# Layer 2's bias table, repeated 16 times in device memory and read with falling offsets, in place of products with a reversing matrix

## The chip, the cores and the metric

The kernel runs on one core of a Trainium2 chip. The metric is device time in microseconds (us), the median of several runs. TensorE (PE) does matrix products into PSUM, VectorE (DVE), ScalarE (ACT) and GpSimd (Pool) work on SBUF, and SyncE (SP) issues nearly all DMAs.

## The reference

A sequence of four layers is computed for 16 batches of 128 tokens, 256 wide: an attention with a gate (layer 0), an attention of each token to three neighbouring rows of the context (layer 1), a self-attention and a cross-attention with a relative position bias (layer 2), and a state space block with a cross-attention (layer 3). The change concerns only the bias of layer 2:

```python
def rel_pos_bias(emb, num_q, num_k):
    ...
    rel = k_pos[None, :] - q_pos[:, None]
    ...
    bucket = ret + jnp.where(n < max_exact, n, val_large)
    bias = emb[bucket]
    return jnp.transpose(bias, (2, 0, 1))[None]
...
sim = jnp.einsum('bhnd,bhmd->bhnm', q, k)
sim = (sim + rel_pos_bias(rel_emb, n, m)) * SCALE
```

The bias depends on key position minus query position alone, so of each head there are 2 * 128 - 1 = 255 numbers, and query row q holds 128 of them, from place 127 - q on. There are 16 heads in the self-attention ("sa") and 16 in the cross-attention ("ca"), so 32 rows of 255. It is the same for all batches, and the kernel works it out once.

## The kernel before

One batch is one tile of 128 partitions by 256. The work of a batch is cut into four parts (`PART1` is layers 0 and 1, `PART2` the self-attention, `PART3` the cross-attention, `PART4` layer 3), each a list of named stages. Each engine has its own program, and its order is written by hand: `HEAD` for the opening, in which batches 0 to 3 fill the pipeline, `ORDER` for the loop, `TAIL` for the end. In `HEAD` each letter takes the next stage of one part of one batch: "o" of batch 0's part 1, with the stages of `OPENING` in it, "b" part 1 of batch 1, "e" part 1 of batch 2, "a" part 2 of batch 0. An engine goes through its stages in this order and waits at semaphores, so what stands behind a waiting instruction waits too. A matrix product in float32 shows as two matmuls in the profile.

The bias is made in the opening. The stage `bias_rows` multiplies the embedding with a matrix of zeros and ones on TensorE (L591) and VectorE copies the result to 32 partitions of 255 numbers, `rows_at` (L1155). SP writes it to device memory (L523), waits for it, and reads it back (L525) into `skewed` so that partition p gets each row from place p on: offsets that rise with the partition. Wanted are falling ones. So the eight stages `bias0` to `bias7`, put one each behind eight stages of batch 0, multiply a bank of 512 columns with a reversing matrix ("flip", L601) into `Pc` or `Pd`, and VectorE copies the bank to `bias` (L1160).

What stands around it and is named further on:

- SP, in this order: the table's write and read, the loads of the self-attention's weights Wsaq, Wsakv and Wsao (4 MB), then `store_kv(1)` (L471), which writes the keys and values of batch 0 to `kv_rows`, the index and tokens of batch 2, `store_kv` for batch 1, and the weights of the later layers. All are DMAs of one queue.
- Pool, in this order: `gather` (L1528) of batch 0, an indirect DMA that waits until `kv_rows` has been written and takes three neighbouring rows for each token; `rms0` (L1501 and L1502), the reciprocal root for the norm at the end of layer 0; `rms1`.
- Batch 0 in layers 0 and 1, on TensorE and VectorE: W0o, the gate with W0g, the turn of out0 (`back0`), the scaling L1250 that waits for `rms0`, the centre product L677, the turn (`turn1`), W1q, L1265, and then the attention to the three rows on VectorE, from L1272, which needs the gathered rows, to L1287; the turn L568 of its result, ScalarE's copy of it (o1T), W1o and the sum L1295.

Of the kernel before, what the change touches and what calls it, by code (L numbers as in the profile page):

```python
# [7 lines left out]
B, T, D = 16, 128, 256  # L8
P = 128
# [3 lines left out]
H2, HD2 = 16, 64  # L13
# [7 lines left out]
BUCKETS = 32  # L21
UNIT = 1024
BANK = 512
HU = UNIT // T
# [5 lines left out]
F32 = mybir.dt.float32  # L30
# [7 lines left out]

_SETUP = [("buckets", 2 * T - 1), ("flip", P)]

# [41 lines left out]
def bias_constants():  # L82

    d = np.arange(2 * T - 1) - (T - 1)
    n = np.abs(d)
    far = 8 + sum((n * n >= 64 * 2 ** k).astype(int) for k in range(1, 8))
    bucket = 16 * (d >= 0) + np.where(n < 8, n, far)
    c = np.zeros((P, SETUP_W), np.float32)  # L90
    c[:BUCKETS, SETUP_AT["buckets"][0]:SETUP_AT["buckets"][1]] = np.arange(BUCKETS)[:, None] == bucket[None, :]
    c[:, SETUP_AT["flip"][0]:SETUP_AT["flip"][1]] = np.eye(P)[::-1]
    return c
# [16 lines left out]

FLIPS = 2 * 2 * HU * T // BANK
OPENING = PART1[:2] + ["bias_rows", "fold1"] + PART1[2:]
for _g, _stage in enumerate(("attn0", "gate0", "back0", "center0", "turn1", "near_q", "near_k", "turn_o1")):
    OPENING.insert(OPENING.index(_stage) + 1, f"bias{_g}")

# [11 lines left out]
HEAD = {  # L127
    "PE": "obooobobooboooobobobobooooboooobooobeeabbeabaaebaebeaecdeddadacdaedacecdcdeccdecececdecegigfihfgifghgihgifighfgifiihfffihgifgffhgihiihfhifif",
    "Activation": "oooboobobobobobbobobaeebaaebeedaecadadeacaddccededcceccdcefgfgifghgfiifhigfighgifihigfighhfhihfif",
    "DVE": "oobooboobobbboooooooooobooooobooeaeabebbeaebbbeabddadaaddedacdeccecceceeeedecihifhgifiifhgffigfggfgffifhffifhhffihiifiiigihf",  # L130
    "Pool": "oooboobobbaaebedadceeexdgfhifhffiiiih",
# [15 lines left out]
def merged(order, own, parts):  # L147
# [14 lines left out]

    "prep_exp", "prep_done", "bias_ps", "bias_sb", "skewed_in",

# [23 lines left out]
def build(nc, tokT, ctx, idx, pad, cols, rows, consts, setup, rel, w0_q, w0_k, w0_v, w0_o, w0_g, w1_q, w1_kv, w1_o,  # L188
          wsa_q, wsa_kv, wsa_o, wca_q, wca_kv, wca_o, wm_in, wm_out, w3_q, w3_k, w3_v, w3_o, bias_rows, kv_rows, kv_rows2, out):
    with ExitStack() as stack:  # L190
# [110 lines left out]

        GW = 2 * 2 * HU * T
        skewed = A4[:, 0:GW]
        rows_at = A4[0:2 * H2, GW:GW + 2 * T - 1]
        set_at = A4[:, GW + 2 * T:GW + 2 * T + SETUP_W]
        rel_at = A4[0:BUCKETS, GW + 2 * T + SETUP_W:GW + 2 * T + SETUP_W + 2 * H2]

# [145 lines left out]
        def _(sp):  # L453
# [65 lines left out]
            for m in work1:  # L519
                for a in (0, EDGE + T):  # L520
                    sp.dma_start(m.kv_rows.ap()[a:a + EDGE], Q2["sa"][0:EDGE, 0:2 * D]).then_inc(sem["kv_out"], 16)
            sp.wait_ge(sem["bias_sb"], 1)
            sp.dma_start(bias_rows.ap(), rows_at).then_inc(sem["skewed_in"], 16)  # L523
            sp.wait_ge(sem["skewed_in"], 16)
            sp.dma_start(skewed.rearrange("p (h k) -> p h k", k=T),  # L525
                         bass.AP(tensor=bias_rows, offset=0, ap=[[1, P], [2 * T - 1, 2 * H2], [1, T]])).then_inc(
                             sem["skewed_in"], 16)
            weights("wsa_in", zip(W2["sa"], (wsa_q, wsa_kv, wsa_o)))
# [31 lines left out]
        def _(pe):  # L560
# [27 lines left out]
            def bias_table(t):  # L588
# [3 lines left out]
                          stop=True).then_inc(sem["bias_ps"], 1)  # L592

            def bias_part(g):
                def run(t):
                    if g == 0:
                        pe.wait_ge(sem["skewed_in"], 2 * 16)
                    if g >= 2:
                        pe.wait_ge(sem["bias_sb"], g)
                    a = SETUP_AT["flip"]  # L600
                    pe.matmul((Pc, Pd)[g % 2], set_at[:, a[0]:a[1]], skewed[:, g * BANK:(g + 1) * BANK], start=True,  # L601
                              stop=True).then_inc(sem["bias_ps"], 1)
                return run


# [289 lines left out]
            def project3(t):  # L895
# [4 lines left out]
            stages = {  # L900
                "bias_rows": [bias_table], **{f"bias{g}": [bias_part(g)] for g in range(FLIPS)},
                "kv0": [project0],
# [206 lines left out]
        def _(dve):  # L1109
# [46 lines left out]

            def bias_part(g):
                def run(t):
                    dve.wait_ge(sem["bias_ps"], g + 2)
                    dve.tensor_copy(bias[:, g // 4, g % 4 // 2, g % 2 * BANK:(g % 2 + 1) * BANK],  # L1160
                                    (Pc, Pd)[g % 2]).then_inc(sem["bias_sb"], 1)
                return run

            def held():

                dve.sem_inc(sem["dve_chain"], 1)
                steps[0] += 1

            def softmax_low(t, L, w, p, scores, extra):

                need_unit(t, f"{L}_scores", w)
                held()
                for h in range(HU):
                    at = slice(h * T, (h + 1) * T)
                    ins = dve.tensor_tensor_reduce(p[:, at], scores[:, at], extra(h), 1.0, TOP, ALU.add, ALU.min,  # L1175
                                                   sm(part_of(t, L), "nm", w * HU + h, w * HU + h + 1))
                    if h % (HU // 2) == HU // 2 - 1:
                        ins.then_inc(sem[f"{L}_lows"], 1)
# [261 lines left out]
            def result3(t):  # L1440
# [5 lines left out]
            stages = {  # L1446
                "bias_rows": [bias_table], **{f"bias{g}": [bias_part(g)] for g in range(FLIPS)},
                "inputs": [inputs], "kv0": [project0],
# [236 lines left out]
```

## Time and profile before

| | |
|---|---|
| runs | 1284.43, 1286.72 and 1281.44 us, median 1284.43 |
| span of the profiled execution | 1284.9 us (no time of it is listed beside the span) |
| busy | PE 1225.8, DVE 883.1, ACT 770.2, POOL 332.6 us |
| TensorE's mean granted clock | 0.985 of full speed |
| device memory | 37.64 MB read, 6.35 MB written |

The span goes from the first instruction to the last. Busy times overlap, since the engines run side by side; what counts is the chain of work that ends last.

### The profile page before, as it was taken

What the parts mean: (1) busy time and instruction counts of PE and PEld (TensorE: products, weight loads), DVE (VectorE), ACT (ScalarE), POOL (GpSimd) and SP (SyncE); (2) the same over time, 40 slices, a digit from 0 to 9 for tenths busy, and PEclk for the clock granted to TensorE, in tenths of its full rate; (3) what the DMA queues carried; (4) which work ended last, traced back from release to release, by engine and by line L of the source; (5) the groups of instructions that cost most, each with busy time, mean ns of one, the idle gap of its engine ahead of it and who ended that gap; (6) DMA issues with size and microseconds to landing.
All of it is one profiled execution on the core that took longest, in us unless ns stands there. A gap on an engine that the chain in (4) does not pass through costs nothing.

```text
span 1284.9 us, 27988 instructions
## 1 busy us (share of the span) xinstructions
PE 1225.8 (95%) x9644; PEld 988.3 (77%) x9644; DVE 883.1 (69%) x3414; ACT 770.2 (60%) x2658; POOL 332.6 (26%) x750
## 2 busy tenths in 40 slices
PE   5899899999999999999999999999999999999887
PEld 3568687788788787788788788878878787788665
DVE  4674667687686768678686867768676876836464
ACT  3447457565766756576775757576575655655533
POOL 2111441312314141222314131231414123112150
PEclk9899899999999999999999999999999999999899
DMA  7730001001010100001010100101010010000000
GB/s 219 290 120 13 34 2 43 13 11 44 0 49 4 49 4 25 28 8 45 0 49 4 44 9 8 45 0 49 4 49 4 16 37 34 5 6 1 9 1 13
DMA packets 28620, 44.67 MB, mean 35 GB/s; under 512 B 4716, under 2 KB 20620, under 8 KB 28056
## 3 DMA queue, kind: packets, MB, share of 16 engines
q1 hardware_dynamic: 26264, 31.42, 7.4%
q0 software_dynamic: 2304, 12.58, 2.7%
q8 instruction: 29, 0.48, 0.1%
q14 instruction: 23, 0.19, 0.0%
HBM read 37.64 MB, written 6.35 MB: 34 GB/s over the span
## 4 chain that ended last, share of the span: by engine, by line
PE 89%; DVE 5%; ACT 2%; issue 1%; DMA 1%; POOL 1%; SPq 0%; DVEq 0%; POOLq 0%
PE psum L574 57%; PE psum L568 11%; PE psum L759 5%; PE psum L782 4%; PE psum L625 3%; PE psum L821 2%; PE psum L876 1%; PE psum L836 1%; PE psum L647 1%; PE psum L916 1%; PE psum L677 1%; ACT A L938 1%; PE psum L891 1%; DVE A L1175 1%; ACT A L930 0%
## 5 line engine op out<-in xcount | busy, mean ns | idle before, releaser
L938 ACT ACTIVATE A<-A,small_ 128x128 f32<-128x128 f32 x640 | 248.5, 396 | 49.6 <-DVE small_ L1175 49.6
L930 ACT ACTIVATE A<-psum 128x512 f32<-128x512 f32 (+2 forms) x231 | 155.7, 700 | 173.7 <-PE psum L568 152.9
L568 PE MATMUL psum<-cst,A 128*128 128x128 f32 x888 | 131.5, 281 | 20.8 <-DVE A L1287 6.9
L568 PEld LDWEIGHTS psum<-cst,A 128*128 128x128 f32 x888 | 101.9, 143 | 43.8 <-issue 14.5
L938 ACT ACTIVATION_READ_ACCUMULATOR A<-A,small_ 128x1 f32 x640 | 125.0, 195 | 0.0
L1501 POOL TENSOR_SCALAR small_<-small_ 128x1 f32<-128x1 f32 x96 | 22.6, 236 | 370.1 <-DVE small_ L1189 203.7
L1175 DVE CUSTOM_DVE_ANT_0 A<-psum,cst 128x128 f32<-128x128 f32 x256 | 56.7, 287 | 66.6 <-PE psum L625 66.4
L1175 DVE CUSTOM_DVE_ANT_0 A<-psum,bias 128x128 f32<-128x128 f32 x264 | 58.4, 287 | 63.3 <-PE psum L759 63.3
L1185 DVE TENSOR_TENSOR A<-A,small_ 128x1024 f32<-128x1024 f32 x80 | 98.3, 1229 | 2.7
L938 ACT ACTIVATE sa_p<-sa_p,small_ 128x128 f32<-128x128 f32 x248 | 96.1, 398 | 4.3 <-DVE small_ L1175 4.3
L1366 DVE SCALAR_TENSOR_TENSOR A<-psum,half_cw,A 128x127 f32<-128x127 f32 (+2 forms) x270 | 70.7, 344 | 32.0 <-ACT A L1062 32.0
L1615 POOL TENSOR_TENSOR small_<-small_,neg_half 128x1 f32<-128x1 f32 x16 | 9.0, 565 | 316.8 <-DVE small_ L1408 316.8
L574 PEld LDWEIGHTS psum<-A,Wmi 128*128 128x128 f32 x600 | 69.3, 192 | 9.2 <-issue 9.1
L1175 DVE DVE_READ_ACCUMULATOR2_ANT small_<- 128x1 f32 x896 | 74.8, 83 | 0.1
L574 PE MATMUL psum<-A,Wmi 128*128 128x128 f32 x600 | 74.4, 279 | 0.0
L1502 POOL TENSOR_TENSOR small_<-small_,neg_half 128x1 f32<-128x1 f32 x96 | 59.2, 617 | 8.0
L946 ACT ACTIVATE A<-psum,col 128x128 f32<-128x128 f32 x94 | 38.0, 462 | 36.8 <-PE psum L568 36.7
L574 PE MATMUL psum<-A,Wcaq 128*128 128x128 f32 x480 | 56.3, 275 | 0.0
L574 PE MATMUL psum<-Wcao,A 128*128 128x256 f32 x240 | 56.2, 388 | 0.0
L574 PE MATMUL psum<-A,Wcakv 128*128 128x128 f32 x480 | 56.2, 275 | 0.0
L574 PEld LDWEIGHTS psum<-A,Wcaq 128*128 128x128 f32 x480 | 54.9, 192 | 0.5 <-ACT A L946 0.5
L574 PEld LDWEIGHTS psum<-A,Wcakv 128*128 128x128 f32 x480 | 54.8, 192 | 0.1
(314 smaller groups left out, 2886.8 us busy)
## 6 DMA issues: line engine op xcount, KB each, us to landing
kv_rows<-A SPq DMA_DIRECT2D x16, 256.0 KB
IN<-in_tokT SPq DMA_DIRECT2D x15, 256.0 KB, 2.6
A<-bias_rows SPq DMA_DIRECT2D x1, 2048.0 KB, 10.0
Wsakv<-in_wsa_kv SPq DMA_DIRECT2D x1, 2048.0 KB, 11.6
Wcakv<-in_wca_kv SPq DMA_DIRECT2D x1, 2048.0 KB, 12.8
ctx_end<-in_tokT SPq DMA_DIRECT2D x16, 128.0 KB, 2.2
out<-x_out SPq DMA_DIRECT2D x16, 128.0 KB, 1.7
IN<-in_ctx SPq DMA_DIRECT2D x15, 128.0 KB, 2.0
```

The lines of the kernel that those rows point to most:

```text
L568: mm = pe.transpose(out[:, c * P:(c + 1) * P], src[:, c * P:(c + 1) * P], ident)
L574: mm = pe.matmul(out, lhs[k], rhs[k], start=(k == 0), stop=(k == len(lhs) - 1))
L625: mm = pe.matmul((m.Pa, m.Pb)[r], m.q0o[rows, w * T:(w + 1) * T], m.bk0[rows, :], start=True, stop=True)
L759: mm = pe.matmul(X[:, at:at + T], Q2[S][64 * e:64 * e + 64, a:a + T], K2[S][64 * e:64 * e + 64, a:a + T], start=True, stop=True)
L782: mm = pe.matmul(X[64 * e:64 * e + 64, at:at + T], V2[S][:, h * HD2:(h + 1) * HD2], (Q2, K2)[w][S][:, (4 * e + c) * T:(4 * e + c + 1) * T] ...
L930: return act.activation(out, in_, ACT.Copy)
L938: ins = act.activation(p[:, h * T:(h + 1) * T], p[:, h * T:(h + 1) * T], ACT.Exp, scale=-1.0, bias=sm(part, "nm", w * HU + h, w * HU + h + 1),
L946: ins = act.activation(out[:, k * T:(k + 1) * T], src[:, k * T:(k + 1) * T], ACT.Identity, bias=pc(shift, k), scale=pc(scale, k))
L1175: ins = dve.tensor_tensor_reduce(p[:, at], scores[:, at], extra(h), 1.0, TOP, ALU.add, ALU.min, sm(part_of(t, L), "nm", w * HU + h, w * HU ...
L1185: dve.tensor_tensor(heads(p), heads(p), each(rc, T), ALU.mult).then_inc(sem[f"{L}_probs"], 1)
L1366: ins = dve.scalar_tensor_tensor(to, m.P_4[:, c * T:(c + 1) * T - d], half_cw[:, c * TAPS + TAPS - 1 - d:c * TAPS + TAPS - d], to, ALU.mul ...
L1502: pool.tensor_tensor(out, t, neg_half[:, 0:1], ALU.pow).then_inc(sem[name], 1)
```

## The change

The table is written to device memory 16 times over, so that each of the 32 rows stands there 16 times one behind another (`WRAP` = 16). A row is 255 numbers long. Going from partition to partition by 254 numbers, which is one copy further and one number back, gives offsets that fall with the partition, for 16 partitions at a time. Eight DMAs, one for each group of 16 partitions, put the bias straight into `bias`. The reversing matrix, the eight products and the eight copies are gone, and VectorE waits for the eight DMAs ahead of the first softmax of the self-attention.

```diff
-_SETUP = [("buckets", 2 * T - 1), ("flip", P)]
+_SETUP = [("buckets", 2 * T - 1)]
...
-FLIPS = 2 * 2 * HU * T // BANK
+WRAP = 16
 OPENING = PART1[:2] + ["bias_rows", "fold1"] + PART1[2:]
-for _g, _stage in enumerate(("attn0", "gate0", "back0", "center0", "turn1", "near_q", "near_k", "turn_o1")):
-    OPENING.insert(OPENING.index(_stage) + 1, f"bias{_g}")
...
-            sp.dma_start(bias_rows.ap(), rows_at).then_inc(sem["skewed_in"], 16)
-            sp.wait_ge(sem["skewed_in"], 16)
-            sp.dma_start(skewed.rearrange("p (h k) -> p h k", k=T),
-                         bass.AP(tensor=bias_rows, offset=0, ap=[[1, P], [2 * T - 1, 2 * H2], [1, T]])).then_inc(
-                             sem["skewed_in"], 16)
+            sp.dma_start(bias_rows.ap(), rows_at.unsqueeze(1).to_broadcast([2 * H2, WRAP, 2 * T - 1])).then_inc(sem["table_out"], 16)
+            sp.wait_ge(sem["table_out"], 16)
+            flat = bias[:].rearrange("p a w n -> p (a w) n").rearrange("p a (h k) -> p (a h) k", k=T)
+            for a in range(0, P, WRAP):
+                sp.dma_start(flat[a:a + WRAP], bass.AP(tensor=bias_rows, offset=T - 1 - a,
+                                                       ap=[[2 * T - 2, WRAP], [WRAP * (2 * T - 1), 2 * H2], [1, T]])).then_inc(
+                                                           sem["bias_in"], 16)
             weights("wsa_in", zip(W2["sa"], (wsa_q, wsa_kv, wsa_o)))
...
             def softmax_low(t, L, w, p, scores, extra):
 
                 need_unit(t, f"{L}_scores", w)
+                if L == "sa" and w == 0 and t.first:
+                    dve.wait_ge(sem["bias_in"], P // WRAP * 16)
...
-    bias_rows = nc.dram_tensor("bias_rows", (2 * H2, 2 * T - 1), F32)
+    bias_rows = nc.dram_tensor("bias_rows", (2 * H2, WRAP, 2 * T - 1), F32)
```

The functions `bias_part` of TensorE and VectorE are taken out with their stages, and `HEAD` loses eight letters "o" for each of the two engines. The other stages keep their order.

Line numbers shift with the change (L525 becomes L522, L494 L489, L471 L466, L574 L571). On SP's queue, between the small stores that clear the edges of `kv_rows` and the tokens of batch 2, there stood:

```order
L523 DMA bias_rows<-A 32x255
L525 DMA A<-bias_rows 128x32x128
L494 DMA Wsaq<-in_wsa_q 128x2x1024
L494 DMA Wsakv<-in_wsa_kv 128x2x2048
L494 DMA Wsao<-in_wsa_o 128x8x256
L471 DMA kv_rows<-A 128x512
```

and now, with the semaphores that SP waits for:

```order
L518 DMA bias_rows<-A 512x1x255 [waits bias_sb]
L522 DMA bias<-bias_rows 16x32x128 [waits table_out]
L522 DMA bias<-bias_rows 16x32x128 x7
L489 DMA Wsaq<-in_wsa_q 128x2x1024
L489 DMA Wsakv<-in_wsa_kv 128x2x2048
L489 DMA Wsao<-in_wsa_o 128x8x256
L466 DMA kv_rows<-A 128x512 [waits kv1_sb]
```

One read of 128 partitions has become eight of 16, all ahead of the three Wsa loads and of the store of keys and values.

On TensorE, from batch 1's product with W1kv (its `kv1`) to the gate product of batch 1, there stood:

```order
L574 MATMUL psum<-W1kv,A 128x512 [waits folded]
L574 MATMUL psum<-W1kv,A 128x512
L601 MATMUL psum<-A 128x512 [waits bias_sb]
L677 MATMUL psum<-A,cst 128x256 [waits y0]
L601 MATMUL psum<-A 128x512 [waits bias_sb]
L568 MATMUL psum<-cst,A 128x128 [waits x1]
L568 MATMUL psum<-cst,A 128x128
L574 MATMUL psum<-A,W0o 128x128 [waits l0_osb,w0_in]
L574 MATMUL psum<-A,W0o 128x128 x3
L601 MATMUL psum<-A 128x512 [waits bias_sb]
L574 MATMUL psum<-W1q,A 128x256 [waits x1gT]
L574 MATMUL psum<-W1q,A 128x256
```

and now:

```order
L571 MATMUL psum<-W1kv,A 128x512 [waits folded]
L571 MATMUL psum<-W1kv,A 128x512
L662 MATMUL psum<-A,cst 128x256 [waits y0]
L565 MATMUL psum<-cst,A 128x128 [waits x1]
L565 MATMUL psum<-cst,A 128x128
L571 MATMUL psum<-A,W0o 128x128 [waits l0_osb,w0_in]
L571 MATMUL psum<-A,W0o 128x128 x3
L571 MATMUL psum<-W1q,A 128x256 [waits x1gT]
L571 MATMUL psum<-W1q,A 128x256
```

The three products with the reversing matrix are gone from between; nothing else has moved.

## Rows read from the trace of the kernel before

**Rows 1.** The page: span, TensorE's busy time, and what the DMAs moved in 40 slices.

```profile
span 1284.9 us, 27988 instructions
...
PE 1225.8 (95%) x9644; PEld 988.3 (77%) x9644; DVE 883.1 (69%) x3414; ACT 770.2 (60%) x2658; POOL 332.6 (26%) x750
...
GB/s 219 290 120 13 34 2 43 13 11 44 0 49 4 49 4 25 28 8 45 0 49 4 44 9 8 45 0 49 4 49 4 16 37 34 5 6 1 9 1 13
```

**Rows 2.** The instructions of L601 and of L1160: durations (ns), starts (us).

```profile
L601 PE MATMUL psum<-A x16: 592/592/1061, 42.0 to 64.1; 128*128 128x512 f32 x16
...
L1160 DVE COPY bias<-psum x8: 684/692/693, 43.1 to 65.2; 128x512 f32<-128x512 f32 x8
```

**Rows 3.** The chain of work up to 110 us: start us, us, what.

```profile
5.62 5.16 DMA A<-in_rel
...
42.19 0.86 PE psum L601 x2
...
55.53 0.87 PE psum L601 x2
...
60.23 0.69 DVE bias L1160
...
63.45 1.71 PE psum L601 x2
...
66.90 0.43 DVE x L1295
...
75.92 11.64 PE psum L574 x76
```

**Rows 4.** Timeline of SP from 20 us: start us, us, operation.

```profile
20.07 0.31 SPq L523 DMA_DIRECT2D bias_rows<-A  x1
21.54 0.39 SPq L525 DMA_DIRECT2D A<-bias_rows  x1
...
28.04 0.49 SPq L494 DMA_DIRECT2D Wsao<-in_wsa_o  x1
42.42 0.34 SPq L471 DMA_DIRECT2D kv_rows<-A  x1
```

**Rows 5.** DMA issues from 20 to 46 us: last number, us to landing.

```profile
A<-bias_rows SPq DMA_DIRECT2D x1, 2048.0 KB, 10.0
...
Wsao<-in_wsa_o SPq DMA_DIRECT2D x1, 1024.0 KB, 14.5
...
bias_rows<-A SPq DMA_DIRECT2D x1, 31.9 KB, 1.5
...
A<-kv_rows,near_at POOLq DMA_INDIRECT x1, 5.0
```

**Rows 6.** DMA issues from 40 to 60 us, the same columns.

```profile
IN<-in_tokT SPq DMA_DIRECT2D x1, 256.0 KB, 2.7
```

**Rows 7.** The page's DMA issues, medians over the whole span.

```profile
out<-x_out SPq DMA_DIRECT2D x16, 128.0 KB, 1.7
```

**Rows 8.** Timeline of Pool from 40 us; in brackets idle time before, and releaser.

```profile
45.38 1.23 POOL L1528 DMA_INDIRECT A<-kv_rows,near_at  x1 [18.60 <-DMA kv_rows<-A]
49.51 0.18 POOL L1501 TENSOR_SCALAR small_<-small_ 128x1 f32<-128x1 f32 x1 [2.90 <-ACT A L978]
```

**Rows 9.** Timeline of all engines from 43 to 76 us.

```profile
48.62 1.88 PE L574 MATMUL psum<-W1kv,A 128*128 128x512 f32 x4
...
57.03 0.95 DVE L1272 TENSOR_TENSOR A<-A 128x768 f32<-128x768 f32 x1
...
62.76 0.69 PE L568 MATMUL psum<-cst,A 128*128 128x128 f32 x2 [3.73 <-DVE A L1287]
```

**Rows 10.** Windows of 2 us: busy us (count) by engine, granted clock, DMA share, GB/s.

```profile
60.00:62.00 2.00, 0.00 (x0) 0.00 (x0) 1.93 (x4) 0.00 (x0) 0.00 (x0) 1.00 0.96 400
...
64.00:66.00 2.00, 2.00 (x5) 1.21 (x4) 1.56 (x4) 0.00 (x0) 0.00 (x0) 0.50 1.07 370
...
68.00:70.00 2.00, 2.00 (x16) 1.95 (x14) 1.46 (x5) 0.00 (x0) 1.74 (x5) 0.79 1.00 396
```

More of the change, by code:

```diff
@@ L91, in bias_constants @@
     c[:BUCKETS, SETUP_AT["buckets"][0]:SETUP_AT["buckets"][1]] = np.arange(BUCKETS)[:, None] == bucket[None, :]
-    c[:, SETUP_AT["flip"][0]:SETUP_AT["flip"][1]] = np.eye(P)[::-1]
     return c
@@ L127 @@
 HEAD = {
-    "PE": "obooobobooboooobobobobooooboooobooobeeabbeabaaebaebeaecdeddadacdaedacecdcdeccdecececdecegigfihfgifghgihgifighfgifiihfffihgifgffhgihiihfhifif",
+    "PE": "oboooboboobooobobbobooboboobeeabbeabaaebaebeaecdeddadacdaedacecdcdeccdecececdecegigfihfgifghgihgifighfgifiihfffihgifgffhgihiihfhifif",
     "Activation": "oooboobobobobobbobobaeebaaebeedaecadadeacaddccededcceccdcefgfgifghgfiifhigfighgifihigfighhfhihfif",
-    "DVE": "oobooboobobbboooooooooobooooobooeaeabebbeaebbbeabddadaaddedacdeccecceceeeedecihifhgifiifhgffigfggfgffifhffifhhffihiifiiigihf",
+    "DVE": "oobooboobobbboooooboooboeaeabebbeaebbbeabddadaaddedacdeccecceceeeedecihifhgifiifhgffigfggfgffifhffifhhffihiifiiigihf",
     "Pool": "oooboobobbaaebedadceeexdgfhifhffiiiih",
@@ L161 @@
     "const_in", "w0_first", "w0_in", "w1_in", "wsa_in", "late_in",
-    "prep_exp", "prep_done", "bias_ps", "bias_sb", "skewed_in",
+    "prep_exp", "prep_done", "bias_ps", "bias_sb", "table_out", "bias_in",
     "kv0", "q0", "l0_o", "attnT", "gateT", "out0", "x1c", "x1T", "kv1", "q1", "o1T", "y1",
@@ L300, in build @@
         pad_at = xc[:, 0:T].bitcast(I32)
[L302 to L306, printed above, removed]
+        rows_at = A4[0:2 * H2, 0:2 * T - 1]
+        set_at = A4[:, 2 * T:2 * T + SETUP_W]
+        rel_at = A4[0:BUCKETS, 2 * T + SETUP_W:2 * T + SETUP_W + 2 * H2]
         def C(name, p=P):
@@ L592, in bias_table @@
                           stop=True).then_inc(sem["bias_ps"], 1)
[L594 to L603, printed above, removed]
             def project0(t):
@@ L900, in _ @@
             stages = {
-                "bias_rows": [bias_table], **{f"bias{g}": [bias_part(g)] for g in range(FLIPS)},
+                "bias_rows": [bias_table],
                 "kv0": [project0],
@@ L1155, in bias_table @@
                 dve.tensor_scalar(rows_at, Pd[0:2 * H2, 0:2 * T - 1], -HD2 ** -0.5, None, ALU.mult).then_inc(sem["bias_sb"], 1)
[L1157 to L1162, printed above, removed]
             def held():
@@ L1446, in _ @@
             stages = {
-                "bias_rows": [bias_table], **{f"bias{g}": [bias_part(g)] for g in range(FLIPS)},
+                "bias_rows": [bias_table],
                 "inputs": [inputs], "kv0": [project0],
```

## The prediction

> **What bounds the kernel now.** I read the page first: the span is 1284.9 us and TensorE is busy for 95% of it [rows 1]. The change touches only the opening, so the next view is the chain of work up to 110 us. From 75.92 on it is TensorE with hardly a break: there a shift of the start is carried to the end, neither grown nor made good. Before that the chain is one of short steps on TensorE, VectorE, ScalarE and Pool, with loads between them, and the removed work stands on it: five pieces of L601, 0.86 or 0.87 us each, the first at 42.19 and the last at 55.53, one of 1.71 us at 63.45, and one copy of L1160 (0.69 us) at 60.23 [rows 3]. All of L601 is 16 passes of 592 ns, and L1160 is eight copies of 692 ns [rows 2]; what doesn't lie on the chain gives nothing. On the chain stand 4.31 + 1.71 + 0.69 = 6.7 us. That is the most that the removal can give, and 0.5% of the whole, which is also about what a measurement of this kernel can tell from no change.
>
> The second thing to see is the queue. SP issues the table's write at 20.07, the read of 2 MB at 21.54, the last Wsa load at 28.04 and the store of batch 0's keys and values at 42.42 [rows 4]. The read lands 10.0 us after its issue, at 31.5, and the last load 14.5 us after its own, at 42.5 [rows 5]: the load's data had just left the queue when the store was issued. Then Pool: it sits 18.6 us until that store has landed, issues the gather at 45.38, and only behind it, in its own order, computes the reciprocal root at 49.51 [rows 8]. So whatever delays the store holds up not only the gather but every step from 49.51 on.
>
> **The change, part by part.**
>
> *The smaller setup load.* 128 rows of 383 numbers become 255, 65.5 KB less ahead of the in_rel load that the chain waits for until 10.8 us [rows 3]. At the 219 GB/s of the first slice [rows 1] that is 0.3 us, all on the chain. A gain of 0.3; it could be none.
>
> *Products and copies taken out.* I walk the chain with them gone. The piece at 42.19 gives about 0.55, since the gate's products behind it wait for VectorE as well. Between the Pool step at 49.51 and L1272 at 57.03 [rows 8, 9] lie four pieces and one copy, 4.1 us in all; I take half of it, 2.1, because the centre product and the turn each wait for a VectorE step that the pieces partly cover, while the piece between W0o and W1q and the copy ahead of L1272 count in full. The stretch shrinks from 7.5 to 5.4. The copy at 60.23 gives 0.7. Between the turn at 62.76 and the sum at 66.90 [rows 3, 9] the piece of 1.71 gives 0.9, for ScalarE's copy of o1T has to be made in that time anyway. In all 0.3 + 0.55 + 2.1 + 0.7 + 0.9 = 4.6 us, if no load comes late.
>
> *The table's write.* It was 32 KB and landed in 1.5 us [rows 5]; now it is 16 times that, 522 KB. Nearest above is a store of 128 KB that lands in 1.7 us [rows 7]; four of them make 6.9. Bounds 1.5 and 6.9; I take 3.8, nearer the middle, since little else is in the queues then. Issued at 19.8 it has landed at 23.6, and SP waits for that.
>
> *The reads.* One read of 2 MB to 128 partitions becomes eight of 256 KB, each to 16 partitions. The lower bound is the one read's own 10.0 us: the same 4096 pieces of 512 bytes. The upper bound is eight loads one behind another: a load of 256 KB lands in 2.7 us [rows 6], so 21.6. No row shows a load to 16 partitions. I take 20.0, near the upper bound, since each is in size that load, and since all the pieces that are under way at one moment now go to sixteen neighbouring partitions. With 20.0 the bias lands at 43.7.
> The Trainium skill speaks against the change here. Its page "SBUF — State Buffer", section "Door 1: The DMA port swizzle", says that the bandwidth of a DMA depends on how many of 16 ports its partitions reach, that 16 neighbouring ones reach four, and that 104 GB/s was measured so. By it a read would take 2.5 us and the eight 20; by the row of the one read, 10.0.
>
> *What stands behind them.* The Wsa loads landed 11.0 us behind the old read (42.5 less 31.5 [rows 4, 5]) and are needed only at 75.92 [rows 3], so they hide their own delay. They land at 54.7. The store of keys and values is behind them in the same queue: with the 1.7 us of a store [rows 7] it lands at 56.4 in place of 45.4. The seven further issues cost SP some 3 us and nothing else, since it stood idle until 42.42. VectorE's new wait for the bias stands ahead of its first use, which comes behind the products that start at 75.92; the bias has been there for 30 us by then.
>
> *What waits for the store.* Pool issues the gather at 56.4 (1.3 us), then takes the root; 5.4 us further on L1272 starts, at 63.1 in place of 57.03. The gather itself lands 5.0 us behind its issue [rows 5], at 61.5, and is covered. That is 6.1 us late; less 0.7 and 0.9 for what is removed behind it, 4.5.
>
> *The clock.* TensorE ends the W1kv product of batch 1 at 50.5 [rows 9] and would then stand idle to about 59. Before, an idle stretch of 3.7 us up to 62.76 [rows 9] was followed by a granted clock of 0.50, the 1.2 GHz level, back at 2.4 GHz only in 68 to 70 [rows 10]. So I expect the centre product, turn, W0o and W1q, 2.4 us at the full clock, to take twice that, and give back 0.8 because the clock may be up again where it was halved before: 1.6. Sum: 4.5 + 1.6 = 6.1 us, that is 1291.0 against the span of 1284.9. The page lists no time of that execution beside its span; the median of the runs is 1284.43, 0.5 lower, so I forecast 1290.5.
>
> **The rivals.**
> *Reads partly side by side* (12 to 17 us in all). For it: SP issues one every 0.4 us, and nothing orders them on the chip but the engines they share. With 14 the store lands at 50.4, L1272 starts at 57.1, and the removed 1.6 stand against about 1 us of clock: 1284 or so; 1282 to 1288 over the range.
> *Reads as quick as the one read*: bytes and pieces are the same. The bias lands at 33.7 and Wsa at 44.7; the store lands at 46.4, before Pool is wanted at about 49.0. The whole 4.6 less a little: 1280.1. This is the other side. It decides if the reads take less than about 11 us; with 15 the gain is gone.
> *All removed pieces count*, 6.7 + 0.3, with the idle stretches too short for the clock to fall: 1277.4. Against it: the 3.7 us before 62.76 are VectorE's and remain.
> *More late than I reckon*: the write at its bound, the reads at 21.6, and the gather beside the late weights. The store lands at 61, and another 5 us come on top: 1295.
>
> **How the numbers follow.** Reads one after another 0.45 (own range 1287.5 to 1293.5), partly side by side 0.22, as quick as before 0.24, all pieces 0.04, more late 0.05. The first stands over the third because the new reads differ from the old one in what they write to, and are like the load of 256 KB in size; the third has the same pieces of 512 bytes for it. The range 1279.5 to 1294.0 leaves out the two outer ones and the tail of the third. Slower than 1290.9 is somewhat over half of the first and the last: 0.30. Faster than 1278.0: 0.07, the all-pieces case and a little of the quick one. Within: 0.63.
>
> **What would show it.** The landings of the new reads: the last 20 us behind the first's issue, against 8 to 10. The store of keys and values landing at 56 rather than 46, and Pool's gather issued then. Pool's root at 58, not 49. An idle TensorE from 50 to 59 with the clock at 0.50 behind it, against none before 55. The in_rel load 0.3 us earlier. From 76 on the two traces should differ by a constant. The prediction is wrong if 16 neighbouring partitions are written as fast as 128, or if something that I take for hidden (the Wsa loads, the tokens of batch 2) is reached first.

## The result, and the profile after

The changed kernel takes 1295.28 us, the median of 4 runs from 1294.34 to 1297.25; the kernel before takes 1284.45 beside it (4 runs, 1281.44 to 1286.72). The ratio is 1.0086, with an interval of 1.0066 to 1.0107: slower, by 10.8 us. That lies 4.8 us above the forecast of 1290.5 and 1.3 above the upper end of the range.

The page of the changed kernel, the span and TensorE's row:

```profile
span 1293.3 us, 27954 instructions
...
PE 1222.7 (95%) x9628; PEld 987.1 (76%) x9628; DVE 877.2 (68%) x3406; ACT 768.5 (59%) x2658; POOL 333.3 (26%) x750
```

TensorE and VectorE have less to do than in [rows 1], 3.1 and 5.9 us less, and the span is 8.4 us longer. The timeline of SP shows where that begins:

```profile
20.85 0.68 SPq L518 DMA_DIRECT2D bias_rows<-A  x1
25.61 8.11 SPq L522 DMA_DIRECT2D bias<-bias_rows  x8
...
36.60 1.46 SPq L489 DMA_DIRECT2D Wsao<-in_wsa_o  x1
44.05 5.31 SPq L466 DMA_DIRECT2D kv_rows<-A  x1
```

The DMA issues from 18 to 80 us (last number: median us to landing):

```profile
bias<-bias_rows SPq DMA_DIRECT2D x8, 256.0 KB, 9.9
...
Wsao<-in_wsa_o SPq DMA_DIRECT2D x1, 1024.0 KB, 19.2
...
bias_rows<-A SPq DMA_DIRECT2D x1, 510.0 KB, 4.7
...
A<-kv_rows,near_at POOLq DMA_INDIRECT x1, 4.8
```

The table's write lands in 4.7 us where it was 1.5 [rows 5]. The reads begin 4.8 us behind it, in place of 1.5 [rows 4]. The chain of work:

```profile
5.63 6.00 DMA A<-in_rel
12.81 2.70 DMA A<-in_tokT
...
44.05 12.36 DMA kv_rows<-A
56.48 0.64 issue
57.35 1.23 POOL A L1508
58.93 0.59 POOL small_ L1482
59.55 0.49 DVE A L1230
...
66.55 0.97 DVE A L1252
...
74.96 0.43 DVE x L1275
...
75.53 3.77 PE psum L571 x16
...
86.01 11.64 PE psum L571 x76
```

The store of keys and values of batch 0 needs 12.36 us to land, because the reads and 4 MB of weights are ahead of it in the queue. Pool starts the gather at 57.35 (45.38 in [rows 8]), and the reciprocal root comes behind it. The attention to three rows starts at L1252 at 66.55 (L1272 at 57.03 in [rows 9]), the sum x is at 74.96 (66.90 in [rows 3]), and the product that closes the opening at 86.01 (75.92). So the delay is 9.5, 8.1 and 10.1 us at these three places. TensorE's timeline shows what it waits for and how long its products are:

```profile
49.58 1.88 PE L571 MATMUL psum<-W1kv,A 128*128 128x512 f32 x4
60.08 1.22 PE L662 MATMUL psum<-A,cst 128*128 128x256 f32 x2 [8.62 <-DVE A L1230]
...
62.30 1.91 PE L571 MATMUL psum<-A,W0o 128*128 128x128 f32 x8
64.01 1.91 PE L571 MATMUL psum<-W1q,A 128*128 128x256 f32 x4
...
77.23 2.05 PE L571 MATMUL psum<-IN,W0q 128*128 128x128 f32 x8
80.08 2.08 PE L610 MATMUL psum<-A,IN 64*128 64x512 f32 x4 [0.80 <-DVE IN L1195]
```

TensorE stands idle for 8.62 us ahead of the centre product. The windows give the granted clock (us, busy us and count by engine, clock, DMA share, GB/s), first the reads, then the two halved stretches:

```profile
28.00:42.00 14.00, 10.88 (x66) 7.00 (x64) 8.05 (x44) 10.82 (x50) 0.00 (x0) 1.00 1.25 131
58.00:66.00 8.00, 5.40 (x18) 4.32 (x19) 2.30 (x7) 0.51 (x2) 3.68 (x8) 0.50 0.85 282
72.00:82.00 10.00, 8.55 (x28) 5.66 (x26) 5.94 (x18) 0.86 (x3) 3.83 (x9) 0.50 1.05 383
```

Behind the idle stretch the clock is at its lower level, 1.2 GHz, from 58 to 66 and, after the wait for the attention to three rows, again from 72 to 82 (before, behind the same wait, it was back at 2.4 GHz in 68 to 70 [rows 10]). Longer windows, of before and then of the changed kernel:

```profile
20.00:70.00 50.00, 39.91 (x218) 24.12 (x216) 33.71 (x124) 21.66 (x85) 12.62 (x22) 0.86 0.81 290
70.00:120.00 50.00, 47.63 (x389) 37.82 (x388) 28.12 (x133) 32.65 (x116) 4.35 (x11) 1.00 0.11 38
120.00:170.00 50.00, 43.10 (x315) 35.98 (x314) 31.25 (x101) 22.06 (x76) 23.04 (x27) 0.93 0.07 25
```

```profile
20.00:70.00 50.00, 32.16 (x179) 20.25 (x178) 23.10 (x100) 20.76 (x82) 10.76 (x17) 0.90 0.93 232
70.00:120.00 50.00, 45.95 (x305) 34.57 (x306) 30.47 (x115) 26.77 (x95) 6.43 (x15) 0.86 0.27 101
120.00:170.00 50.00, 41.69 (x351) 34.97 (x350) 30.13 (x109) 25.57 (x91) 19.58 (x19) 1.00 0.09 30
```

Before lost clock between 120 and 170 us, the changed kernel did not. Two steps of VectorE, of before and then of the changed kernel, show what that does to the distance between the two:

```profile
145.19 0.48 DVE L1265 TENSOR_SCALAR A<-psum,small_ 128x256 f32<-128x256 f32 x1 [1.88 <-PE psum L574]
160.17 0.42 DVE L1295 TENSOR_TENSOR x<-A,psum 128x256 f32<-128x256 f32 x1 [5.52 <-PE psum L574]
```

```profile
155.18 0.48 DVE L1245 TENSOR_SCALAR A<-psum,small_ 128x256 f32<-128x256 f32 x1 [1.72 <-PE psum L571]
168.64 0.42 DVE L1275 TENSOR_TENSOR x<-A,psum 128x256 f32<-128x256 f32 x1 [3.84 <-PE psum L571]
```

It is 10.0 us at the first and 8.5 at the second. So the 10.1 us at the close of the opening are 8.4 at the end of the span.

### The profile page after: what moved, and what is told of

Same layout as the page of the kernel before. It is cut to its first block, busy times and chain, and to the rows that moved or that the text cites. A ratio compares the mean times of both kernels' runs of the same rounds, so it can differ in the third digit from the quotient of the medians.

```text
span 1293.3 us, 27954 instructions
## 1 busy us (share of the span) xinstructions
PE 1222.7 (95%) x9628; PEld 987.1 (76%) x9628; DVE 877.2 (68%) x3406; ACT 768.5 (59%) x2658; POOL 333.3 (26%) x750
## 4 chain that ended last, share of the span: by engine, by line
PE 88%; DVE 5%; ACT 3%; DMA 2%; issue 1%; POOL 1%; SPq 0%; DVEq 0%; POOLq 0%
PE psum L571 57%; PE psum L565 11%; PE psum L744 5%; PE psum L767 4%; PE psum L610 3%; PE psum L806 2%; PE psum L821 1%; PE psum L632 1%; ACT A L923 1%; PE psum L861 1%; DMA kv_rows<-A 1%; PE psum L901 1%; PE psum L662 1%; PE psum L876 1%; DVE A L1155 1%
## 5 line engine op out<-in xcount | busy, mean ns | idle before, releaser
L571 PEld LDWEIGHTS psum<-A,Wmi 128*128 128x128 f32 x600 | 69.3, 192 | 9.2 <-issue 9.1
L571 PE MATMUL psum<-A,Wmi 128*128 128x128 f32 x600 | 74.4, 279 | 0.0
L571 PE MATMUL psum<-A,Wcaq 128*128 128x128 f32 x480 | 56.3, 275 | 0.1
L571 PE MATMUL psum<-A,Wcakv 128*128 128x128 f32 x480 | 56.1, 275 | 0.0
L571 PEld LDWEIGHTS psum<-A,Wcaq 128*128 128x128 f32 x480 | 54.8, 192 | 0.5 <-ACT A L931 0.5
L571 PEld LDWEIGHTS psum<-A,Wcakv 128*128 128x128 f32 x480 | 54.8, 192 | 0.1
L1155 DVE CUSTOM_DVE_ANT_0 sa_p<-psum,bias 128x128 f32<-128x128 f32 x240 | 53.0, 286 | 2.0 <-PE psum L744 1.3
## 6 DMA issues: line engine op xcount, KB each, us to landing
Wcakv<-in_wca_kv SPq DMA_DIRECT2D x1, 2048.0 KB, 12.5
```

The costliest lines, as they stand in the source:

```text
L571: mm = pe.matmul(out, lhs[k], rhs[k], start=(k == 0), stop=(k == len(lhs) - 1))
```

## The experiments

Two theories stood at first. One: the eight reads are slow because each goes to 16 neighbouring partitions; the store of keys and values stands behind them in the queue, and Pool and TensorE wait for it. The other: the reads cost what they do because there are eight of them, or because of the table they read, or the loss is not the reads at all. All ratios are to the kernel before, run on the same chip.

| kernel | reads | gather issued | ratio [interval], runs | median, us |
|---|---|---|---|---|
| before | one, 128 partitions | 45.38 | | 1284.45 |
| changed | eight of 16 neighbours | 57.35 | 1.0086 [1.0066, 1.0107], 4 | 1295.28 |
| e1 | the same, behind the store | 47.53 | 0.9993 [0.9979, 1.0008], 10 | 1283.77 |
| e2 | eight of 16, 8 apart | 50.65 | 1.0022 [1.0011, 1.0034], 10 | 1288.68 |
| e3 | eight of 128, table of 16 copies | 77.38 | 1.0234 [1.0217, 1.0251], 4 | 1315.39 |
| e4 | one of 128, plain table | 44.58 | 0.9986 [0.9976, 0.9996], 10 | 1283.82 |
| e5 | changed, 22 spare products | | 1.0066 [1.0044, 1.0088], 4 | 1293.26 |
| e7 | e1, 10 spare products | | 0.9952 [0.9935, 0.9969], 7 | 1279.38 |
| e8 | one of 128, table of 16 copies | 68.71 | one run | 1308.29 |
| e9 | eight of 128, plain table | 46.15 | one run | 1287.17 |
| e10 | e2 behind the store, 10 spare | | 0.9968 [0.9956, 0.9981], 11 | 1280.72 |
| e11 | before, 10 spare products | | 0.9995 [0.9981, 1.0009], 11 | 1283.58 |
| e12 | changed, root ahead of gather | 57.44 | 1.0112 [1.0089, 1.0135], 4 | 1297.3 |
| e13 | e4, 10 spare products | | 0.9972 [0.9961, 0.9983], 10 | 1280.0 |
| e14 | eight of 16 neighbours, plain table | 54.83 | one run | 1289.72 |
| e15 | e12, late weights held back | 57.34 | 1.0043 [1.0028, 1.0058], 9 | 1291.71 |

The chips differ: before has medians of 1284 to 1286 us, and its single runs go from 1280 to 1289. So the three single runs are read for what their traces show of the reads, not for their time. The traces differ at the start too: the load of in_rel, which the chain waits for, ends anywhere from 10.1 us (e8) to 12.5 (e1), so a place in one trace can be set against the same place in another only to about 1 or 2 us.

**The place of the reads (e1).** The loop of L522 is moved down in SP's program, behind the load of the context of batch 2 and ahead of the weights of the later layers:

```diff
-            for a in range(0, P, WRAP):
-                sp.dma_start(flat[a:a + WRAP], ...
             weights("wsa_in", ...)
             store_kv(1)
...
+            for a in range(0, P, WRAP):
+                sp.dma_start(flat[a:a + WRAP], ...
```

> The changed kernel with its eight reads issued later on SP, behind the load of batch 2's context and ahead of the late weights; nothing else differs. Theory A (the reads are slow, and what costs time is that the keys and values of batch 0 stand behind them in the queue): the store lands near 46 us instead of 56, Pool's root comes at 49 to 50, TensorE has no idle stretch of 8 us, and the removed products show: 1280.5 us, 4 below the kernel before. The reads themselves still take 15 us or more in all. Theory B (the time was lost elsewhere, for example in the repeated write or in VectorE's new wait): no more than 2 us off the changed kernel's 1295.3. Theory C (the reads hurt wherever they stand, because the second gather and the late weights now meet them): the store is in time but the sum is 1285 to 1290.

Pool in e1:

```profile
47.53 1.23 POOL L1508 DMA_INDIRECT A<-kv_rows,near_at  x1 [19.66 <-DMA kv_rows<-A]
```

The loss is gone. The reads are as slow as ever (153 and 161 GB/s while they run, from 55 to 66), but only weights of later stages stand behind them. Pool's root comes at 51.01, L1252 at 56.46, 5.45 us later; the prediction had 5.4 for that stretch with the products taken out, against 7.5 before. Of the gain of some 4 us that the removal should then leave, nothing is measured (1283.77, where theory A had 1280.5). Part of it is seen to go in the opening: from the sum x to the product with Wsaq e1 needs 12.25 us (64.88 to 77.13), and before needed 9.02, with the clock halved from 62 to 76.

**The partitions (e2).** The same eight reads, each to 16 partitions that are 8 apart:

```diff
-            for a in range(0, P, WRAP):
-                sp.dma_start(flat[a:a + WRAP], bass.AP(..., ap=[[2 * T - 2, WRAP], ...
+            for a in range(P // WRAP):
+                sp.dma_start(flat[a:P:P // WRAP], bass.AP(..., ap=[[2 * T - 1 - P // WRAP, WRAP], ...
```

> The eight reads stand where they stood, but each writes 16 partitions that lie 8 apart instead of 16 neighbours; the same number of DMAs, pieces and bytes, from the same 16 copies. Theory A1 (sixteen neighbouring partitions are what makes them slow): the rate of 130 GB/s goes up to twice that, the last read lands about 10 us behind the first one's issue instead of 18, and the kernel takes 1281 to 1284 us. Theory A2 (eight DMAs of 256 KB pay a fixed time each): no difference, 18 us and 1295. Theory A3 (reading from 0.5 MB of copies instead of from one table of 32 KB is slow): no difference, 18 us and 1295.

The median landing falls from 9.9 to 6.0 us. The DMA issues, Pool, and the window from 28 to 36:

```profile
bias<-bias_rows SPq DMA_DIRECT2D x8, 256.0 KB, 6.0
```

```profile
50.65 1.23 POOL L1508 DMA_INDIRECT A<-kv_rows,near_at  x1 [23.81 <-DMA kv_rows<-A]
```


```profile
28.00:36.00 8.00, 5.15 (x36) 2.81 (x36) 6.94 (x40) 6.70 (x32) 0.00 (x0) 0.79 1.23 218
```

218 GB/s in place of 131, with the same bytes, pieces and table. The gather is issued 6.7 us earlier, TensorE's idle time ahead of the centre product is 4.07 us and not 8.62, and the loss falls from 0.86% to 0.22%. The rate did what theory A1 said, the time did not: it had 1281 to 1284, and 1288.68 was measured. In the trace the sum x comes at 67.73, 0.8 us behind [rows 3], but from there to the product with Wsaq it takes 12.25 us, as in e1.

**Eight or one, plain table or copies (e3, e9, e14, e8).** The first of these left the question more open than before, and the others take it apart. e3 splits by rows, four rows to all partitions:

```diff
-            for a in range(0, P, WRAP):
-                sp.dma_start(flat[a:a + WRAP], ...
+            for a in range(0, 2 * H2, 4):
+                sp.dma_start(flat[:, a:a + 4], bass.AP(tensor=bias_rows, offset=a * WRAP * (2 * T - 1),
+                                                       ap=[[1, P], [WRAP * (2 * T - 1), 4], [1, T]])).then_inc(
```

> Eight reads of 256 KB again in the same place, but each brings four of the 32 rows to all 128 partitions, with offsets that rise (the reversal is left out, so each query gets the bias of the mirrored one). Theory A1 (neighbouring partitions): about 8 to 10 us for all eight, the store near 47 us, 1280 to 1283 in all. Theory A2 (a fixed time for each DMA): 18 us and 1295. Theory A3 isn't tested by it, since only the first of the copies is read.

It was by far the slowest, and neither theory had that: a median landing of 17.5 us, and the gather issued at 77.38. e3 still read from the table of 16 copies, in which its rows are 16 KB apart and all partitions of a row read in the first copy. e9 is e3 with a table that is written once (32 KB, rows next to each other):

```diff
-            sp.dma_start(bias_rows.ap(), rows_at.unsqueeze(1).to_broadcast([2 * H2, WRAP, 2 * T - 1]))...
+            sp.dma_start(bias_rows.ap(), rows_at)...
-                ... offset=a * WRAP * (2 * T - 1), ap=[[1, P], [WRAP * (2 * T - 1), 4], [1, T]]
+                ... offset=a * (2 * T - 1), ap=[[1, P], [2 * T - 1, 4], [1, T]]
```

> Eight reads to 128 partitions of four rows each, from the table written once with its rows packed (the reversal is left out). Theory S (how the source lies): the eight take 8 to 12 us together. Rival N (the number of DMAs, or four rows at a time, wherever they lie): 30 us or more, as with the rows 16 KB apart.

e14 is e9 with the split of the change, 16 neighbouring partitions and all 32 rows:

```diff
-                sp.dma_start(flat[:, a:a + 4], ... ap=[[1, P], [2 * T - 1, 4], [1, T]]
+                sp.dma_start(flat[a:a + 16], ... ap=[[1, 16], [2 * T - 1, 2 * H2], [1, T]]
```

> Eight reads to 16 neighbouring partitions each, as in the changed kernel, but from the table written once with its rows packed in 32 KB (offsets rise, so the reversal is left out). It takes the source out of the question. Theory A1 (the sixteen neighbouring partitions written to set the rate): 130 GB/s again, all eight landed 16 to 18 us behind the first's issue. Rival S (copies that lie apart are slow to read, as the rows 16 KB apart were at 82 GB/s): near the one wide read, 9 to 11 us for all eight.

e8 is one read to 128 partitions from the table of copies:

```diff
-                                       ap=[[1, P], [2 * T - 1, 2 * H2], [1, T]])).then_inc(sem["bias_in"], 16)
+                                       ap=[[1, P], [WRAP * (2 * T - 1), 2 * H2], [1, T]])).then_inc(sem["bias_in"], 16)
```

> One read to 128 partitions, as in the bare removal, but from the first of the 16 copies of each row, so that the 32 rows lie 16 KB apart instead of 1 KB (the reversal is left out). It looks for why eight wide reads of four rows moved only 50 GB/s. Theory S (rows that lie far apart, few of them at a time, are slow to read): the read takes 30 us or more. Rival N (the number of DMAs): 9 to 10 us, as with the rows packed.

The DMA issues of e9 and its window of 24 to 30 us:

```profile
bias<-bias_rows SPq DMA_DIRECT2D x8, 256.0 KB, 4.7
```

```profile
24.00:30.00 6.00, 4.21 (x13) 1.62 (x12) 4.91 (x32) 5.12 (x27) 1.82 (x6) 1.00 1.03 283
```

Of e14, and its window of 26 to 36:

```profile
bias<-bias_rows SPq DMA_DIRECT2D x8, 256.0 KB, 10.2
```

```profile
26.00:36.00 10.00, 6.76 (x38) 3.07 (x35) 8.42 (x54) 8.07 (x38) 1.08 (x3) 0.75 1.25 119
```

Of e8:

```profile
bias<-bias_rows SPq DMA_DIRECT2D x1, 2048.0 KB, 32.6
```

Between e9 and e14 only the split differs: 283 GB/s to 128 partitions, 119 to 16 neighbours. So neither the number of DMAs nor the table makes the change's reads slow; the partitions do. The table's write has a smaller part in the late store: with 32 KB written in place of 510, e14 issues the gather at 54.83, 2.5 us ahead of the changed kernel, of the 12.0 us by which that one is late. And between e8 and e4 (9.2 us) only the table and its write differ: the very read that took 10.0 us [rows 5] takes 32.6 when its rows are 16 KB apart. So the table has a cost of its own, but in another pattern than the change's: the change's rows are as far apart, and its partitions read from different copies, and its rate (131) is no lower than e14's. What in the memory makes the pattern of e3 and e8 slow wasn't tried.

**What the removal is worth (e4, e13, e11).** e4 is the bare removal, with the table and the one read of before, straight into `bias`:

```diff
+            sp.dma_start(flat, bass.AP(tensor=bias_rows, offset=0,
+                                       ap=[[1, P], [2 * T - 1, 2 * H2], [1, T]])).then_inc(sem["bias_in"], 16)
```

> Only the removal of the eight products and eight copies: the table is written once (32 KB) and read with one DMA to 128 partitions, as in the kernel before, but straight into the bias (the reversal is left out). Theory A: this is what the removal is worth with no load made later: 4.3 us, so 1280.1, with TensorE's first long idle stretch again the one of 3.7 us ahead of the turn of o1. Rival: the removed products filled time in which TensorE waited anyway, so 1283 to 1285; another rival: all that stood on the chain counts, 6.7 us, 1277.7.

It gives 0.14%, 1.8 us, where the prediction had 4.6; of e4's own three forecasts, the rival's 1283 to 1285 was met. In its trace W1o takes 2.07 us, the length at 1.2 GHz, and the clock falls once more in the product with Wsaq, which starts 4.7 us ahead of [rows 3] but takes 12.81 us for 11.64. e13 adds ten products whose result nobody reads, ahead of the turn of batch 0's layer 1, where TensorE waits 3.88 us for VectorE (e7 and e10 have the same lines, e11 the same products into another part of PSUM):

```diff
+                if t.first:
+                    for _ in range(10):
+                        pe.matmul(Pc[:, 0:D], ident, cst[:, 0:D], start=True, stop=True)
```

> The bare removal (one read to 128 partitions straight into the bias, reversal left out), which took 1283.8 us, with the 10 spare products ahead of the turn of o1. If the clock is what the removed products had been giving back, 1279.5 us, the same as with the later reads and the spare products; if there is still something else in the way of the 4.3 us, 1282 or more.

> The kernel before with the same 10 spare products ahead of batch 0's turn of o1, to tell what of the gain is the spare products' and what the change's. Its trace shows the clock halved for 6.6 us behind that idle stretch, on work of some 4 us at the full clock with 1.7 us of the removed product in it. Theory A: 1281.5 to 1282.5 us, 2 to 3 below the kernel before, so that the removal itself is worth 2 to 3 more. Rival: the products do nothing here, 1284.5, and the gain needs both.

TensorE's timeline in e13:

```profile
60.66 1.13 PE L569 MATMUL psum<-W1o,A 128*128 128x256 f32 x4 [0.47 <-ACT A L916]
...
70.12 3.84 PE L569 MATMUL psum<-sa_p,Wsaq 128*128 128x128 f32 x32
```

W1o takes 1.13 us, and the product with Wsaq starts 5.7 us ahead of before's. The whole gain is 0.28%, 3.6 us. The two intervals overlap a little, so by this pair alone the spares' part is likely, not certain. The same ten on the kernel before give nothing that can be measured (0.9995), as the rival in e11's forecast had it.

**The clock with the loads out of the way (e7, e10).** e7 is e1 with those ten:

> The kernel with the reads issued later (1283.8 us, 0.7 per mille under the one before) with 10 spare products on TensorE ahead of the turn of o1, where it stands idle for 3.9 us. In that kernel and in the one with the bare removal the granted clock was halved for 20 us of the first 120, against 14 in the trace of before: theory A is that this is where the rest of the removal's 4.3 us went, so with the clock held the time is 1280 to 1281. Rival: the removed products were covered more than the chain of work shows, so nothing changes, 1283.5 to 1284.

Its windows, beside e1's:

```profile
52.00:72.00 20.00, 16.98 (x103) 13.02 (x102) 16.80 (x66) 6.76 (x29) 5.64 (x12) 1.00 1.16 167
```

```profile
52.00:72.00 20.00, 13.73 (x60) 9.85 (x60) 13.71 (x36) 2.68 (x8) 6.00 (x14) 0.73 1.11 171
```

The clock stays at 2.4 GHz, and here the intervals are apart: 0.9952 against 0.9993. This is the fastest kernel of the study, 0.48% under before, with the whole bias computed. e10 joins it with the partitions 8 apart, which should save nothing where nothing waits for the reads:

> The changed kernel with its eight reads 8 partitions apart, issued behind the load of batch 2's context, and 10 spare products ahead of batch 0's turn of o1: the whole computation, and the version that the experiments point to. With the reads out of the way their own rate shouldn't matter, so the same as with neighbouring partitions and the spare products: 1279.5 us, 0.4 to 0.5% under the kernel before. If the second gather or the late weights had been held up by the slower reads, another 1 us less.

0.9968, the same as e7 within their intervals. Both are faster than the kernel before, clear of noise, and than the changed one.

**The clock in the changed kernel (e5).** 22 products like these stand ahead of the centre product, in the idle stretch of 8.62 us.

> The changed kernel with 22 spare products (128x256, a result that nobody reads) on TensorE ahead of the centre product of batch 0, where it stands idle for 8.6 us. They wait for nothing and delay nothing. Theory A (part of the loss is TensorE at 1.2 GHz behind the long wait): the centre product, turn, W0o and W1q take 2.4 us in place of 4.8, and the root-to-L1252 stretch shrinks from 7.9 to 5.4 us; if the clock holds on behind it too, another 1 to 3 us: 1290 to 1293 in place of 1295.3. Rival (the clock is no term, the chain there is VectorE's and Pool's): 1295 as before.

The centre product takes 0.59 us (1.22), W0o 1.06 and W1q 1.03 (1.91 each), and the product with Wsaq starts at 81.54, 4.4 us earlier. At the end of the span 2.6 are left of it (1290.7 beside 1293.3): e5 loses clock between 120 and 170 us, which the changed kernel does not. In the medians it is 2.0 us, 1293.26, and the intervals of e5 and of the changed kernel overlap. So TensorE's clock is a part of the loss in the opening's trace; that it is one in the time is likely, not shown, and by these numbers it isn't the larger part.

**Pool's order (e12, e15).** Is it that the root stands behind the gather? In e12 it is ahead of it, for batch 0:

```diff
             def rms0(t): ...
+                if t.first:
+                    gather_rows(t)
```

> The changed kernel (reads in their place) with one thing moved on Pool: batch 0's reciprocal root for the end of layer 0 ahead of its gather. Theory P (what makes the late store so dear is that the root stands behind the gather's wait): the root comes at 49 to 50 us instead of 58.7, the centre product and W1q are done by 55, and L1252 waits only for the gathered rows, at 62 instead of 66.5: 1290 to 1291 us. Rival (the gathered rows themselves are what is late): the root comes early and L1252 doesn't, 1295.

The centre product starts at 52.16, 8 us earlier, yet nothing is gained (1297.3; theory P had 1290 to 1291). The chain now goes through the gather. VectorE's timeline in e12:

```profile
67.14 0.96 DVE L1252 TENSOR_TENSOR A<-A 128x768 f32<-128x768 f32 x1 [6.41 <-DMA A<-kv_rows,near_at]
```

SP issues the late weights from 58.08 on (60.76 in the changed kernel), the gather is issued at 57.44 and lands 9.7 us later, beside the loads of the late weights (4 MB in the first three). In the changed kernel the same gather takes 4.8 and is covered by the centre product, the turn and the products behind it. e15 lets SP wait for the gather's landing ahead of the late weights:

```diff
+            sp.wait_ge(sem["near_in"], 16)
```

> The kernel with the root ahead of the gather on Pool (1297.3 us), and with SP issuing the late weights only when batch 0's gathered rows have landed. There the gather took 9.7 us in place of 4.8, since the weights were already under way. If that is why moving the root gained nothing, the gather takes 5 us, L1252 starts at 62 to 63 in place of 67.1 and the time is 1291 to 1293. Rival (the gather is slow for another reason, or something else holds L1252): 67 again and 1297.

```profile
62.15 0.96 DVE L1253 TENSOR_TENSOR A<-A 128x768 f32<-128x768 f32 x1 [1.51 <-DMA A<-kv_rows,near_at]
```

The gather lands in 4.8 us, and L1253 starts 5.0 us ahead of e12. The time is 1291.71, as forecast, and the loss falls to 0.43%. So the two moves together recover about half of it. Which part is whose is open, since SP's wait wasn't tried without the move on Pool; the move alone gave nothing. Behind them L1253 still waits for the gathered rows and starts 5.1 us later than in [rows 9]. That this late gather is the other half of the loss is the reading that fits; Pool's order can't mend it while the reads are ahead of the store.

## Why the prediction was off

**Right: the queue.** The store was forecast to land at 56.4 and landed at 56.41 (44.05 + 12.36). That it was met so closely is luck, since two errors cancel in it. The table's write was issued at 20.85, not 19.8, and took 4.7 us, not 3.8, so the reads began at 25.6, not 23.6. They took less than eight single loads would: at 131 GB/s their 2.1 MB take 16.0 us, and with the start-up some 18 by my estimate, to about 43.5, where the forecast had 20.0. The reason that the prediction gave for its 20.0 (16 neighbouring partitions) is what e2, e9 and e14 bear out, and e1 shows that their place ahead of the store is what costs.

The Trainium skill, on its page "SBUF — State Buffer", section "Door 1: The DMA port swizzle", says that 16 neighbouring partitions reach four of 16 ports and that about 104 GB/s was measured so. The direction holds here; the rate in this case is 131 (119 in e14). By the section's formula 16 partitions that are 8 apart reach eight ports, twice as many, and e2 has 218.

**Right: the stretch.** 5.4 us from root to the attention, measured as 5.45 in e1, where the clock is full.

**Wrong: the size.** The forecast for the span was +6.1, and it came to +8.4.

- *"Pool issues the gather at 56.4."* That is when the store lands. Pool's instruction starts 0.95 us later, at 57.35.
- *"The clock ... 1.6."* The first part was right: the centre product, the turn, W0o and W1q were expected to lose 2.4 and lost 2.5. The step that failed is the next one, "give back 0.8 because the clock may be up again where it was halved before". Nothing came back there: the clock fell a second time behind the same wait, W1o took 2.07 us (1.91 before), and it stayed down longer, from 72 to 82. Between x and the product with Wsaq before needed 9.02 us and the changed kernel 11.05: W0q's product 2.05 and not 1.14, L610 2.08 and not 1.13. Those 2.0 are a loss, and 1.7 came back far behind, between 120 and 170 us. 2.5 + 2.0 - 1.7 = 2.8 where 1.6 stood. So "a shift of the start is carried to the end, neither grown nor made good" fails too, by those 1.7. How long the clock stays down behind this wait differs from trace to trace: from x to Wsaq it is 8.4 us in e14, 9.0 before, 11.05 in the changed kernel and 12.25 in e1 and e2, behind waits of 3.5 to 4.0 us. What decides it, the kernel or the single run, is open.
- The start was taken as 0.3 early. The load of in_rel took 6.00 us, not less than the 5.16 of [rows 3], and the tokens were issued at 12.81. In the other traces that load took 4.5 to 6.8, and 5.76 in e11, which has the larger setup load; of the smaller one nothing can be seen in this scatter. Since the store's landing was met, this is within the cancelled errors.

0.95 + 1.2 explain 2.2 of the 2.3 us between 6.1 and 8.4; the rest is the removed work behind L1252, which gave 1.5 (9.87 us from there to x before, 8.41 now) and not 1.6.

**Wrong: from the span to the median.** *"The median of the runs is 1284.43, 0.5 lower, so I forecast 1290.5."* The larger part of the miss is here, 2.5 of 4.8 us. In every run with both numbers the time is 1.8 us above the span (1295.1 beside 1293.3). With that the span of 1284.9 belongs to a run of 1286.7, the highest of the three, and the difference of two profiles (8.4) is 2.4 short of the difference of the medians (10.8). Before's own spans go from 1278.7, at a mean clock of 0.993, to 1287.0. The profiled run had 0.985; the median of the 74 runs of before that were timed beside the experiments is 0.989, and those with more clock are shorter on the whole. So a typical run of before loses less to the clock than the profiled one did; in which stretch, no trace shows. It is also a reason why e4's span is 5.5 us below that of [rows 1] and its median only 1.8 better, by the ratio; the other is that e4's profiled run, 1281.28, is the fastest of its ten.

**The removal** was put at 4.6 us if no load comes late. With the spares that hold the clock (e13) it is 3.6, without them (e4) 1.8. The reading that fits is that the eight products were not only work but also helped to hold the clock: the spares give a gain clear of noise where the products are gone (e7 against e1) and none where they are still there (e11). The forecast had the clock only in the case with late loads, so the rival "as quick as the one read" at 1280.1 was too low as well, by some 2 to 3 us.

**The rivals.** Partly side by side, with the store at 50.4, is what e2 does on purpose: its gather is issued at 50.65, and it comes out 0.22% slower (the rival had 1284). The last rival, "more late than I reckon", has the measured number, 1295, but not by its mechanism: it had the store at 61, which landed at 56.4, and the gather beside the late weights, which did not happen in the changed kernel (4.8 us) but did in e12 (9.7 us).

## What to carry to other kernels

Before putting a transfer on a queue, read what stands behind it there and who waits for that: here eight reads whose data nobody used before 100 us made the kernel 0.86% slower ahead of a small store, and left it as it was behind that store. Work that is taken out between a bottleneck engine's waits may have been holding up its clock; look at the granted clock behind each wait that grows, and price every later stretch, not only the first. Place a profiled run among the timed runs before its span is used as the base of a sum.

## What the runs showed of the hardware

- Reads of 2 MB in pieces of 512 bytes: 131 GB/s to 16 neighbouring partitions at a time and 218 to 16 partitions 8 apart, both from the table of 16 copies; 119 to 16 neighbours and 283 to all 128, both from the plain table.
- The same read of 128 partitions takes 9.2 us from rows next to each other and 32.6 us from rows 16 KB apart, of which each is read by all partitions in one copy (e4, e8). Split into eight by rows it is slower still: the gather behind it is issued at 77.38 us in e3 and at 68.71 in e8.
- SP is held at a DMA's issue: 5.31 us at the store in the changed kernel, with the reads and 4 MB of weights ahead of it, and 0.34 us at the same place before [rows 4].
- An indirect gather that lands in 4.8 us takes 9.7 when large loads are issued just behind it (e12), and 4.8 again when they are held back until it has landed (e15).
